# A graph kernel's top-p search: the root of the threshold is halved, the next tile's search starts a pair earlier, and work around it changes place

## Reference

```python
cs = jnp.cumsum(sp, axis=-1)              # sp: the row, sorted downwards
keep_sorted = cs - sp < TOP_P
...
A = probs * mask
return A / jnp.maximum(A.sum(-1, keepdims=True), 1e-12)
...
for n in range(STEPS):
    A = _top_p_attention(Xa, W1, W2, W3)
    Xf = R @ Xf
    Xa = A @ Xa
    Z = Z + Xf @ U1[n].T + Xa @ U2[n].T
h = X + Z                                 # then a layer norm, plus x, and a second layer norm
```

## Time and profile before

| | |
|---|---|
| median of 3 executions | 1876.28 us (1875.42 to 1879.34) |
| the profiled execution, its own time | 1873.67 us |
| its span, first to last instruction | 1872.0 us |
| granted clock of TensorE, mean | 0.914 |
| ranking and mixing of step 0 | up to about 857 us |
| ranking of step 1, with its last lists | to about 1266 us |
| search of tile 0 | about 1281 to 1355 us |
| sweep | 1364 to about 1862 us |

### The profile page before, as it was taken

How to read it: one execution, slowest core, us unless ns; L and a number is a source line. 1 busy time by engine, 2 the same in 40 slices (tenths; PEclk the granted TensorE clock), 3 DMA queues, 4 the chain that set the end, 5 groups by cost and what they waited for, 6 DMA issues and landing times. The chain is left out here.

```text
span 1872.0 us, 18415 instructions
## 1 busy us (share of the span) xinstructions
PE 1550.3 (83%) x4817; PEld 897.4 (48%) x4817; DVE 1400.4 (75%) x3789; ACT 762.9 (41%) x1182; POOL 247.3 (13%) x264
## 2 busy tenths in 40 slices
PE   6999999931799999999999999941179677867995
PEld 3555555521455555554666665631145343434553
DVE  4777777739477777767999999961879799798564
ACT  3444444421356565655444444421133332323332
POOL 1011111123000000000011111012010421221224
PEclk9999999965799999999999999975589898888997
DMA  6556766500255555555557777700000000000000
GB/s 239 200 183 199 183 181 182 175 1 0 103 200 198 185 185 192 206 208 198 179 172 181 179 179 180 179 3 3 1 3 1 7 1 6 7 6 1 7 6 12
DMA packets 55436, 211.89 MB, mean 113 GB/s; under 512 B 24832, under 2 KB 33600, under 8 KB 34736
## 3 DMA queue, kind: packets, MB, share of 16 engines
q1 hardware_dynamic: 52080, 210.56, 36.4%
q0 software_dynamic: 3264, 0.30, 0.2%
HBM read 206.63 MB, written 4.45 MB: 113 GB/s over the span
## 5 line engine op out<-in xcount | busy, mean ns | idle before, releaser
L1512 DVE MAX8 cand<-psL 128x8 f32<-128x256 f32 (+1 forms) x640 | 372.3, 583 | 95.7 <-PE psL L776 92.2
L1105 ACT ACTIVATE psL<-psL,umax 128x1024 f32<-128x1024 f32 x256 | 278.6, 1088 | 333.5 <-DVE umax L1506 329.5
L775 PE MATMUL psL<-kA,mq 128*128 128x512 f32 x512 | 298.7, 583 | 8.0 <-DVE mq L1339 7.6
L1234 ACT ACTIVATE ebuf<-psL 128x1024 f32<-128x1024 f32 x128 | 131.0, 1023 | 303.1 <-PE psL L952 254.9
L753 PE MATMUL psO<-adj_in,xn 128*128 128x512 f32 x512 | 241.1, 595 | 0.0
L894 PE MATMUL psO<-ebuf,xn 128*128 128x512 f32 x512 | 241.1, 593 | 0.0
L753 PE MATMUL psO<-adj_in,xf 128*128 128x512 f32 x512 | 240.7, 594 | 0.1
L1773 DVE SCALAR_TENSOR_TENSOR ebuf<-ebuf 128x1024 f32<-128x1024 f32 x128 | 156.7, 1224 | 99.6 <-PE psO L894 93.1
L776 PE MATMUL psL<-kB,mq 66*128 66x512 f32 x512 | 203.6, 398 | 0.0
L1171 ACT ACTIVATE ebuf<-psL 128x1024 f32<-128x1024 f32 x128 | 131.0, 1023 | 136.4 <-PE psL L866 136.4
L951 PE MATMUL psL<-mq,kA 128*128 128x512 f32 x256 | 151.7, 593 | 41.1 <-DVEq L1968 41.1
(11 more groups left out here) (366 smaller groups left out, 2178.5 us busy)
## 6 DMA issues: line engine op xcount, KB each, us to landing
adj_in<-in_adjT SPq DMA_DIRECT2D x128, 1024.0 KB, 4.8
adj_in<-in_adj SPq DMA_DIRECT2D x32, 2048.0 KB, 7.8
xaT<-in_xT SPq DMA_DIRECT2D x1, 2048.0 KB, 7.9
xa_dram<-xa SPq DMA_DIRECT2D x8, 256.0 KB, 8.1
out<-t SPq DMA_DIRECT2D x8, 256.0 KB, 2.3
list_dram<-ids,place POOLq DMA_INDIRECT x64
rel_prob<-cut_dram SPq DMA_DIRECT2D x32, 2.0 KB
cut_dram<-ncut SPq DMA_DIRECT2D x16, 2.0 KB, 8.8
```

Source lines behind the costliest of these rows:

```text
L775: nc.tensor.matmul(o, qA[:, t * P:(t + 1) * P], kA[:, c:c + BI], start=True, stop=False)
L1105: nc.scalar.activation(ps[:], ps[:], ACT.Exp, bias=umax[:, bass.ds(i * UB + k, 1)], scale=1.0, accum_out=usum[:, bass.ds(i * UB + k, 1)]). ...
L1234: nc.scalar.activation(raw_unit(n), psL[w % 3][:], ACT.Exp).then_inc(g["slot_read"], 1)
L1512: last = v.max(cand[:, t % 2, at + c * 8:at + c * 8 + 8], psL[(turn + k) % 3][:, c * WIDE:(c + 1) * WIDE])
```

## The change

The threshold is written as upper x root^2, and the root is halved between 0 and 1; constants take the place of POOL's power, and `tile_factors` and `tile_bounds` go. The chord aims ten weights above (`BIAS`); 40 candidates instead of 48 are sorted; the fall-back starts at its first factor, 23 halvings. The steps are numbered 0 to 18 and placed by three tables; five of the next tile's run in the tail of a pair. The tile settles at k = 19 instead of 26, and the flag, POOL's store and ScalarE's cut follow. PREP, the norm work and q/cuts have other units. x is added to z by POOL (`add_x`) instead of PE. In the last block z comes after the ranks, on all engines. In step 1 the x rows are gathered on a semaphore of their own, the references by the column that norm and the bound use. The view of the 16 chunks in step 0 has runs of 32 elements instead of single ones.

```diff
-    NEXT = 48
-    BIAS = 0.12
+    NEXT = 40
+    BIAS = 10.0
...
-    PREP_ROWS, PREP_Q, PREP_LOGITS = 7, 8, 11
+    PREP_ROWS, PREP_Q, PREP_LOGITS = 8, 9, 10
...
-        rest_in = ebuf[:, 0:N // UNIT, :].rearrange("p a b -> p (a b)").rearrange("p (e c) -> p c e", c=N // CHUNK)
+        rest_in = ebuf[:, 0:N // UNIT, :].rearrange("p a b -> p (a b)").rearrange("p (k c e) -> p c k e", k=8, c=N // CHUNK)
...
-                            sp.dma_start(ref_dram[bass.ds(i * BI, BI), :].rearrange("(t p) o -> p (t o)", p=P),
+                            sp.dma_start(ref_dram.rearrange("(p t) o -> p (t o)", p=P)[:, rows],
...
+                def add_x(i, h):
+                    pool.wait_ge(g["r_zo_sb"], 2 * i + h + 1)
+                    pool.sem_inc(met, 1)
+                    rows = slice(i * TB + h * ZT, i * TB + (h + 1) * ZT)
+                    nc.gpsimd.tensor_tensor(t2[:, 0:ZT, :], t2[:, 0:ZT, :], xn[:, rows, :], ALU.add).then_inc(g["r_zx_sb"], 1)
                 assert JQ == TB and PARTS == NB
                 add_self(0)
                 for i in range(NB):
-                    if i < NB - 1:
+                    if i < RING - 1:
                         add_self(i + 1)
+                    if s > 0:
+                        add_x(i, 0)
+                    if RING - 1 <= i < NB - 1:
+                        add_self(i + 1)
+                    if s > 0:
+                        add_x(i, 1)
...
-                        for dst, src, at in ((xgs[:, st, :], source, 0), (hrefs[:, st:st + 1], ref_dram, 0),
-                                             (htops[:, st:st + 1], top_dram[s], 1)):
-                            if src is ref_dram:
-                                pool.wait_ge(g["cut_out"], 64 * NB)
+                        nc.gpsimd.indirect_dma_start(
+                            out=xgs[:, st, :], out_offset=None, in_=source,
+                            in_offset=bass.IndirectOffsetOnAxis(ap=gids[:, st, 0:1], axis=0),
+                            bounds_check=N - 1, oob_is_err=False).then_inc(g["h_x"], 16)
+                        pool.wait_ge(g["cut_out"], 64 * NB)
+                        for dst, src in ((hrefs, ref_dram), (htops, top_dram[s])):
                             nc.gpsimd.indirect_dma_start(
-                                out=dst, out_offset=None, in_=src,
-                                in_offset=bass.IndirectOffsetOnAxis(ap=gids[:, st, at:at + 1], axis=0),
-                                bounds_check=N - 1, oob_is_err=False).then_inc(g["h_x"], 16)
-                    def tile_factors(r, c):
...
-                            scaled(r, 2 * p, 0)
                             if p < PT:
                                 tile_store(r, p + 1)
-                            if p < PAIRS - 2:
-                                tile_factors(r, p + 2)
+                            scaled(r, 2 * p, 0)
...
-                        nc.tensor.matmul(psT[:, 2 * e + 1, :], xaT[:, c:c + P], u_sb[:, 1, 0, :], start=True, stop=False)
-                        last = nc.tensor.matmul(psT[:, 2 * e + 1, :], ident[:], xn[:, i * TB + t, :], start=False, stop=True)
+                        last = nc.tensor.matmul(psT[:, 2 * e + 1, :], xaT[:, c:c + P], u_sb[:, 1, 0, :], start=True, stop=True)
...
+                ranks(NB - 1)
+                pe.wait_ge(g["st_tally"], NB)
                 if s == 0:
                     to_rows(NB - 1)
-                    pe.wait_ge(g["r_n_sb"], NB)
                 else:
                     z_terms(NB - 1, 0)
                     z_terms(NB - 1, 1)
-                    pe.wait_ge(g["r_z_sb"], 2 * NB)
-                ranks(NB - 1)
...
+                            if u == 3 and i % 2 == 1 and p < PT:
+                                tile_flag(r, p + 1)
+                            if u == 5 and i > 0:
+                                if i % 2 == 1 and p < PT:
+                                    pe.wait_ge(g["h_read"], r * PT + p + 2)
                                 mix_last(r, i - 1)
                             if u == PREP_ROWS and ahead:
                                 if i > 0:
...
                                 tile_rows(r, c)
                             if u == PREP_Q and ahead:
                                 tile_q(r, c)
-                            if u == 10 and i % 2 == 1 and p < PT:
-                                pe.wait_ge(g["m_z_add"], r * NB + i)
-                                tile_flag(r, p + 1)
-                            if u == 12 and i < NB - 1:
+                            if u == 10 and i < NB - 1:
                                 if i > 0:
                                     pe.wait_ge(g["m_z_add"], r * NB + i)
-                                if i % 2 == 1 and p < PT:
-                                    pe.wait_ge(g["h_read"], r * PT + p + 2)
                                 mix_q(r, i + 1)
...
                 for n in range(STEPS_REL + STEPS_CUT + STEPS_PLACE):
-                    if s > 0 and n in (STEPS_REL + 4, STEPS_REL + 8):
-                        z_rows(NB - 1, 0 if n == STEPS_REL + 4 else 1)
                     stats_step(NB - 1, n)
...
@@ the search in the sweep; the one of step 0 has the same next_try and chord @@
+                    def next_try(k):
+                        link(v.tensor_scalar(hstep[:], hsums[:, k:k + 1], htarget[:], 2.0 ** -k, ALU.is_ge, ALU.mult))
+                        link(v.scalar_tensor_tensor(out=hroot[:], in0=hstep[:], scalar=-(2.0 ** -(k + 1)), in1=hroot[:],
+                                                    op0=ALU.add, op1=ALU.add))
+                        link(v.scalar_tensor_tensor(out=htry[:], in0=hroot[:], scalar=hupper[:], in1=hroot[:],
+                                                    op0=ALU.mult, op1=ALU.mult))
+                    def chord():
+                        v.scalar_tensor_tensor(out=hparts[:], in0=hsums[:], scalar=htarget[:], in1=hsums[:],
+                                               op0=ALU.is_lt, op1=ALU.mult)
+                        link(v.tensor_scalar(hroot[:], hroot[:], 2.0 ** -(FIRST + 1), None, ALU.add))
+                        v.tensor_reduce(hbelow[:], hparts[:], AX.X, ALU.max)
+                        link(v.tensor_scalar(hspread[:], hsums[:], htarget[:], -LOWEST, ALU.is_lt, ALU.mult))
+                        v.scalar_tensor_tensor(out=hend[:], in0=hroot[:], scalar=hupper[:], in1=hroot[:],
+                                               op0=ALU.mult, op1=ALU.mult)
+                        link(v.tensor_tensor(hspread[:], hspread[:], hsums[:], ALU.max))
+                        link(v.tensor_reduce(hover[:], hspread[:], AX.X, ALU.min))
+                        v.tensor_tensor(habove[:], htarget[:], hbelow[:], ALU.subtract)
                         link(v.tensor_tensor(hover[:], hover[:], hbelow[:], ALU.subtract))
                         link(v.reciprocal(hover[:], hover[:]))
+                        link(v.scalar_tensor_tensor(out=habove[:], in0=hend[:], scalar=-BIAS, in1=habove[:],
+                                                    op0=ALU.mult, op1=ALU.add))
+                        link(v.tensor_tensor(hover[:], habove[:], hover[:], ALU.mult))
+                        link(v.tensor_scalar(hover[:], hover[:], 0.05, -(2.0 ** -FIRST), ALU.max, ALU.mult))
+                        link(v.tensor_tensor(hroot[:], hroot[:], hover[:], ALU.add))
+                        link(v.scalar_tensor_tensor(out=htry[:], in0=hroot[:], scalar=hupper[:], in1=hroot[:],
+                                                    op0=ALU.mult, op1=ALU.mult))
...
                     def cut_rows(r, i):
+                        if i % 2 == 0:
+                            dve.wait_ge(g["norm_in"], r * (PAIRS * 16) + (i // 2 + 1) * 16)
...
+                    def search_step(r, c, n):
+                        if n < 2 * FIRST:
+                            halve(c, 1 + n // 2, n % 2)
+                        if n == 8:
                             chord()
+                        if n in (9, 10):
+                            chord_step(c, n - 9)
+                        if n in (11, 13):
+                            part_sum(c, (n - 11) // 2, ALU.is_lt)
+                        if n in (12, 14):
+                            part_largest((n - 12) // 2)
+                        if n == 15:
                             tile_sort()
+                            for m in range(3):
+                                sort_round(m)
+                        if n == 16:
+                            for m in range(3, NEXT // 8):
+                                sort_round(m)
+                        if n == 17:
                             tile_threshold()
+                        if n == 18:
                             tile_settle(r, c)
+                    FIRST_PAIR = {k: k for k in range(18)}
+                    FIRST_PAIR[19] = 18
+                    BEFORE = {21: 0, 22: 1, 26: 2, 28: 3, 29: 4}
```

(66 more changed lines are left out.)

146 lines of the change are left out of this document (32 added, 114 removed).

## The result

The changed kernel takes 1818.8 us, the median of four executions (1818.11 to 1819.83); the kernel before, run beside it, 1877.8 (1875.42 to 1884.09). The ratio is 0.9681, 95% interval 0.9656 to 0.9706. I had forecast 1838.0 and a range from 1822 to 1857: the kernel is faster than the range allowed. The profiled execution took 1819.05 us with a span of 1817.4, against 1873.67 and 1872.0 before: -54.6, where my terms gave -38.3.

The account below looks back on a forecast made before the run. PE bounds the ranking and the last sweep pair; DVE with its search lengthens the other pairs. Terms -26.1 - 5.5 - 4.8 - 1.9 = -38.3 on 1873.67 gave 1835.4, plus 2.6 to the median 1838.0 us; range 1822 to 1857.

Parts of the forecast that it names:

- the stretch from the ranking to the first search: After the ranking of step 1: lists 3.2 us later, gather of ids moved by the same; whole stretch -1.9 us.
- The last power, at the end: End of the kernel: removing POOL's last power gains 0, as the last store hides it.
- The sweep: Four pairs ending the kernel: five search half-steps move into the tails of pairs 0 and 1; -26.1 us in all.
- The port: DVE operations held up beside POOL's norm products in the sweep: net 0, bounds -11 and +3 us.
- The waits: DVE's waits in sweep pairs 0, 1, 2: 11.4, 12.7, 13.4 us go; 5.0, 5.0, 6.5 return.
- The ranking: Ranking of step 1: adding x on POOL frees PE; -5.5 us over seven blocks, bounds 0 and -6.3.
- Step 0's search: Search of step 0: no power, faster maxima in runs of 32, fewer operations; -4.8 us, bounds -3 and -6.
- z of the last block: End of the ranking: z work of the last block leaves DVE's chain of statistics; -4.0 us.
- (a): Rival for the sweep: waits only move into the new tails; +17 us, 1855 us; chance 0.15.
- (d): Rival for the sweep: new places do nothing, only DVE's sum of work counts; 1861 us; chance 0.05.
- (b): Rival: threshold free of POOL with nothing in its place, and lists not late; 1824 us; chance 0.12.
- (c): Rival: new search misses a threshold, so one tile takes the fall-back; +134 us, 1972 us; chance 0.06.

Follow-up runs that it names:

- e1: Kernel before, with only the store of references laid out by partition and gathered by the second id: 1860.57 us, ratio 0.9886.
- e2: Changed kernel with only the references stored as single elements again and gathered by the first id: 1843.08 us.
- e12: Changed kernel with x added by TensorE again and step 1's store of cuts also laid out in runs (easy rows get other rows' cuts): 1818.7 us.
- e3: Changed kernel with POOL's two additions of x for the last block moved behind the four lists: 1814.48 us.
- e5: Changed kernel with everything in the sweep back in its old units, new search arithmetic kept: 1842.09 us, ratio to before 0.9805.

## Why the prediction was wrong, point by point

**The failed step** is in the part on the stretch from the ranking to the first search: "The gather of ids then starts 14.87 us after the last list; I move it by the same 3.2." I took a gap whose releaser the view doesn't name for a fixed length behind the list. It was a wait for landings, tied to SP's stores and not to the list: e1, e2 and e12 move it by moving only stores. The line of the diff that did this stood in my own excerpt, and I gave it no term, since its bytes are few. Counted from the tally I had +7.2 (3.2, and the 4.0 by which the tally comes sooner); it is -8.8 for the store (e1) and +3.6 for the lists, which go out 7.4 us later and lose half of that, since the stores hide the other half (13.3 us in e1 and 13.6 in e3, against 16.9).

How much this step decides is seen best in e2, the changed kernel without it: 1843.1 us, inside the range of 1822 to 1857, and 40.4 below the median of before in its group, where I had forecast 38.3. That this is so near is in part luck, as e2's executions lie 14 us apart. By the medians the one line is worth 22.9 us (before to e1) to 24.3 (e2 to the changed kernel) of the 59.0.

**Not in the sum at all**: the gap of 5.5 us on DVE ahead of the tally and 1.1 in a block of the ranking. Both came from the same store, as e1, which differs in it alone, has neither. In e1 the blocks, the stretch to the tally and the gather are 1.1, 5.9 and 8.8 us shorter than before, 15.8 together; its profiled execution is only 13.0 shorter because its sweep, by the same code, ran 3.7 longer. So of the profiled 54.6 us some 16 are the store's. By which path it stops DVE and ScalarE is open: the releaser is not in the trace, and no experiment parted late semaphores from late loading of instructions.

**Put at 0 and wrong**: "The last power, at the end, is hidden by the last store: 0." From the last mask to the end of the span it is 34.2 us before, 32.4 after and 32.2 in e5, which has the new arithmetic in the old places. The last store is issued as long after the last mask in both kernels, 23.6 and 23.7 us; before, POOL's power and DVE's two operations on it end 2.2 us after that issue, and the span ends 8.3 us after them. e1, which keeps the power, has 34.2 too. So the power was most likely worth the 1.8 us, though no run takes it out by itself.

**The sweep**: mechanism right, -22.4 from the first to the last mask for -26.1. Within it two sizes were off in opposite ways. The port was not 0: DVE's work fell by 11.1 us in the sweep (379.1 to 368.0), of which the arithmetic is 2.0 (e5: 377.1) and the places 9.1. The threshold's four products gave back 11.0, the half sums 2.6, and the cut rows and masks took 4.5 and 2.9 (sums of the groups of DVE in the sweep); 1.5 of work now lie past the last mask. That lies near the bound of -11 that I named.

The waits, on the other hand, fell by only some 11 us (22.4 less 11.1), where I had 23.7. What returned is PE's wait for the tile's q, 9.4 us in pair 0 and 2.0 in pair 1 (I had 1.7 a pair; the third of the three waits shown above lies past the last mask and was there before), and the longer jump. Pair 2, which by the cuts used here should have come to 108.4, took 111.9; which of its waits did that was not parted.

The Trainium skill's rule on the shared port (SBUF — State Buffer, Who interferes with whom) held: eight maxima at 1507.95, beside POOL's products, took 2.70 us, no more than the 0.34 each of the earlier trace rows. With the 3 us that I had put on it the forecast would have been nearer, at 1835.

**The ranking**: 0.89 a block, 6.2 us, the upper bound; DVE's slack was enough. **Step 0's search**: -4.9 for -4.8, the 16 maxima at 5.32 us for 5.4; executions with this same code up to there differ by 2.4 us, so the close match is partly luck. **z of the last block**: -3.8 for -4.0 (e1: 19.8 us from the last copy to the tally, after: 16.0). **Gather to sweep**: -3.7 for -5.1; the jump of 4.0 behind the flag lies in it, 1.5 before. (The text of the prediction gives 0.3 for sort, chord and halvings there and its sum takes 0.4; that changes nothing.) **Rivals**: (a) and (d) fall with the sweep; of (b), the free port was real (9.1 of the 11), and the lists came in time, but not as (b) has it: they still go out 7.4 us later against the tally, and only the landings were sooner; (c) didn't occur, no half sum of a fall-back is in the trace.

## What to carry to other kernels

Cost a small store by when its semaphore lands and who waits behind it, not by its bytes: 512 elements of 4 bytes landed 8 us late here, and POOL's transfers on another queue landed no earlier. A wait put down to "issue" has a cause all the same; find which semaphores the code waits for at that line before moving it as a constant. And when a plan of units is moved, look first at the wait at the border between blocks: one early hand-over (q and cuts at unit 11) was worth more here than the work moved into the tails (29.3 us against 4.6), and each place was only possible through another.

## What the hardware did that I had not expected

A store of single elements slows engines that don't touch its data: with it, the ranking's blocks of 46.39 us took up to 55.0, and four executions differed by 14 us instead of 2. Jumping over a fall-back of 23 halvings cost DVE 3.7 to 4.0 us in three of four places in the changed kernel and in one of four in e5; over one halving it cost 1.1 to 1.5.
